# An expert's second product in two accumulations side by side, and the result stored in three pieces

## The chip, the cores and the metric
One core of a Trainium2 chip runs the kernel. The metric is the device time of one execution in microseconds. Three executions of the kernel before took 155.20, 155.12 and 154.73 us, a median of 155.12.

## The reference
Two mixture-of-experts layers over 1024 rows of 128 numbers (8 batches of 128). The change lies in the second layer's sparse part. Cut to what matters:

```python
def _L1_ffn_ref(x, Wg, W1, b1, W2, b2):
    xt = x.reshape(n, h)                       # n = 1024 rows of h = 128
    S = sigmoid(xt @ Wg).T                     # 8 experts x 1024 scores
    G, I = top_k(S, k)                         # k = 256 rows for each expert
    ex = xt[I]
    hid = gelu(einsum('ekh,ehf->ekf', ex, W1) + b1[:, None, :], approximate=False)
    out = (einsum('ekf,efh->ekh', hid, W2) + b2[:, None, :]) * G[..., None]
    return zeros_like(xt).at[I].add(out)       # rows of several experts are summed

x = x + _L0_ffn_ref(_L0_cond_ref(x, cond_8, ...), ...)    # first layer
x = x + _L1_ffn_ref(_L1_cond_ref(x, cond_8, ...), ...)    # second layer
```

W1 is 128 x 512 and W2 is 512 x 128 for each expert. All is float32.

## The kernel before
The program is written for each engine by hand, with semaphores between the engines. The first layer and the second layer's conditioning come first; the change touches only what comes after them.

**The second layer's experts.** Each expert takes 256 rows (CAP). Experts 0 to 6 are sparse (SPARSE = 7): their rows are gathered. Expert 7 is dense: it is computed for all 1024 rows in four units of 256 rows (HEAD = 4). `unit` lists these four and then the seven sparse experts, so sparse expert e is unit 4 + e, and the last is unit 10 (UNITS = 11).

For a sparse expert, GpSimd (POOL) gathers the rows into xg in two indirect DMAs (`gather1`, line 448). TensorE turns them (`turn_xg`), ScalarE (ACT) copies them to xgT, and TensorE makes the first product in `up1(n, h)` (line 649): h = 0 gives chunks 0 and 1 of the 512 hidden numbers, h = 1 chunks 2 and 3, each chunk one matmul with 256 columns. ACT applies the gelu to each chunk and writes h1T (line 935), and counts h1T_ready up by one for each chunk. `down_e(n, h)` (line 732) is the second product: for one half h of the 256 rows it waits until h1T_ready says that all four chunks are there, and adds four products, one for each chunk, in one bank. (The profile counts each of these float32 products as two matmuls, so an expert's second product is 16 of them, and an up1 is 4.) The bank comes from `y_bank`, which goes round banks 6, 7 and 1 for the sparse experts. The last matmul of each half counts y1_sent up.

On VectorE (DVE) `score(e, h)` (line 1280) waits for y1_sent, scales a half by its gate and adds the bias, writes y1 and counts y1_kept up. y1_kept tells TensorE that a bank is free and POOL that the half can be stored.

**Where the halves go.** The sparse experts have 14 halves. The first ten (SCATTERS = 10, experts 0 to 4) are written by indirect DMAs from POOL into zeroed planes in DRAM (`add`, line 455), one plane for each expert, and SP loads each plane back as soon as both halves are in it (line 407); VectorE adds the five planes to the result x1 (`take_part`, line 1299, five sums over 1024 columns). The last four halves (SPREADS = 4, experts 5 and 6) go by TensorE: VectorE and ACT split y1 in three bfloat16 parts in turns (`thirds_of`, line 1289, and ACT's loop at line 987), and `spread_out` (line 752) multiplies them with one-hot matrices, 24 matmuls for each half, summed in banks 5 (chunks of rows 0 to 3) and 3 (chunks 4 to 7).

**Order on the engines.** TensorE, for n from 5 to 10: turn the rows of expert n - 3, up1(n, 0), then both halves of down_e(n - 1), then up1(n, 1). For n = 10 both up1 come ahead of down_e(9). After the loop come down_e(10) and spread_out. ACT takes xgT and the gelus in the order of the units. VectorE goes through the experts, for each the bias, two scores, and from expert 5 on the thirds; after expert 0 it adds the dense expert, after expert 2 it makes the one-hot matrices, after expert 4 it takes planes 0 and 1, and after expert 6 planes 2, 3 and 4. Then it adds the two banks, one sum over 512 columns for each (line 1341), and each sum counts out_ready up. SP waits for out_ready and stores one half of the result each time (line 410 on; the helper `load` stands at line 357 in the profile), 256 KB in rows of 512 bytes.

Of the kernel before, what the change touches and what calls it, by code (L numbers as in the profile page):

```python
# [24 lines left out]
P = 128  # L25
T, C = 1024, 128
NC = T // P
# [3 lines left out]
NF = F // P  # L31
# [9 lines left out]
NH = CAP // P  # L41
ROW = C + E
SPARSE = 7
# [14 lines left out]
ALU = mybir.AluOpType  # L58
# [55 lines left out]
def adaln_moe(nc, xT, x, first, second, rows, w1, w2, cond_w, gate_w, v1, c1, v2, consts, out):  # L114
    with ExitStack() as ctx:
# [12 lines left out]
        bank = [ctx.enter_context(nc.psum_tensor(f"bank{i}", [P, 512], F32)) for i in range(8)]  # L128
# [19 lines left out]
        v2_sb = sb("v2_sb", [P, E, NF, C])  # L148
# [6 lines left out]
        def const(name):  # L155
# [78 lines left out]
        x1 = c_tok  # L234
# [43 lines left out]
        h1T = sb("h1T", [P, 2, NF, CAP])  # L278
# [47 lines left out]
        xg_turned, xgT_ready, h1_ready, h1T_ready, gb_ready, y1_kept, y1_sent = (sem(n) for n in (  # L326
            "xg_turned", "xgT_ready", "h1_ready", "h1T_ready", "gb_ready", "y1_kept", "y1_sent"))
# [5 lines left out]
        yd_kept = sem("yd_kept")  # L333
# [3 lines left out]
        GATHERS_AHEAD = SPARSE  # L337
        SCATTERS = NH * SPARSE - SPREADS
        SUM_BANKS = (5, 3)

        CHUNKS = T // CAP
        HEAD = DENSE * CHUNKS
# [5 lines left out]
        def y_bank(n, h):  # L348
            return 6 + n % 2 if n < HEAD else (6, 7, 1)[(NH * (n - HEAD) + h) % 3]
# [5 lines left out]
        def _(sp):  # L355
            def load(dst, src, s):
                sp.dma_start(dst, src).then_inc(s, 16)
# [49 lines left out]
            for e in range(PLANES):  # L407
                sp.wait_ge(added[e], 16 * min(NH, SCATTERS - NH * e))
                load(part[e], plane[e].rearrange("(p c) d -> p (c d)", p=P), part_in[e])
            for g in range(2):  # L410
                sp.wait_ge(out_ready, g + 1)
                load(out.rearrange("(c p) d -> p c d", p=P)[:, 4 * g:4 * g + 4], x1[:, 4 * g:4 * g + 4], out_done)
            sp.wait_ge(out_done, 32)


        @block.gpsimd
# [59 lines left out]
        def _(pe):  # L476
# [255 lines left out]
            def down_e(n, h):  # L732
                dense, e, q = unit[n]
                pe.wait_ge(h1T_ready, 4 * (n + 1))
                if n == 0:
                    pe.wait_ge(row_ready, NC)
                if n == 1:
                    pe.wait_ge(sc_ready, 2)
                if 2 <= n < HEAD:
                    pe.wait_ge(yd_kept, n - 1)  # L740
                if n == HEAD:
                    pe.wait_ge(yd_kept, HEAD)
                if n == HEAD + 1 and h == 0:
                    pe.wait_ge(idx1_ready, SPARSE)
                if NH * (n - HEAD) + h >= 3:
                    pe.wait_ge(y1_kept, NH * (n - HEAD) + h - 2)
                for f in range(NF):
                    mm = pe.matmul(bank[y_bank(n, h)][:, C * h:C * h + C], h1T[:, n % 2, f, P * h:P * h + P],  # L748
                                   v2_sb[:, e, f], start=(f == 0), stop=(f == NF - 1))
                mm.then_inc(y1_sent, 1)  # L750

            def spread_out():
                for n in range(SPREADS):
                    pe.wait_ge(spread_ready, n + 1)
                    pe.wait_ge(last_third, n + 1)
                    for c in range(NC):
                        for k in range(3):
                            mm = pe.matmul(bank[SUM_BANKS[c // 4]][:, P * (c % 4):P * (c % 4) + P],
                                           spread1h[n][:, P * c:P * c + P], thirds[:, n, k],
                                           start=(n == 0 and c % 4 == 0 and k == 0),  # L760
                                           stop=(n == SPREADS - 1 and c % 4 == 3 and k == 2))
                        if n == SPREADS - 1 and c % 4 == 3:
                            mm.then_inc(summed, 1)
# [39 lines left out]
            for n in range(HEAD + 1, UNITS):  # L803
                e = n - HEAD
                if e + 1 < SPARSE:
                    turn_xg(e + 1)
                up1(n, 0)
                if n == HEAD + 1:
                    find_slots(SPARSE - 1)
                if n == UNITS - 1:  # L810
                    up1(n, 1)
                for h in range(NH):
                    down_e(n - 1, h)
                if n < UNITS - 1:
                    up1(n, 1)
            for h in range(NH):
# [4 lines left out]
        def _(act):  # L821
# [161 lines left out]
            def y1_of(n):  # L983
                e, h = (SCATTERS + n) // NH, (SCATTERS + n) % NH
                return y1[:, e % Y1_RING, h]

            for n in range(0, SPREADS, NH):
                for m in range(n, n + NH):
                    act.wait_ge(y1_kept, SCATTERS + m + 1)
                    act.activation(thirds[:, m, 0], y1_of(m), ACT.Copy).then_inc(first_third, 1)  # L990
                for m in range(n, n + NH):
                    act.wait_ge(first_left, m + 1)
                    act.activation(thirds[:, m, 1], left[:, m], ACT.Copy).then_inc(second_third, 1)


        @block.vector
        def _(v):
# [338 lines left out]
                    take_part(1)  # L1336
            for e in range(2, PLANES):
                take_part(e)
            for g in range(2):
                v.wait_ge(summed, g + 1)  # L1340
                v.tensor_tensor(acc[:, 512 * g:512 * g + 512], acc[:, 512 * g:512 * g + 512], bank[SUM_BANKS[g]][:],
                                ALU.add).then_inc(out_ready, 1)

# [46 lines left out]
```

## Time and profile before

| | us |
|---|---|
| median of the runs (154.73 to 155.20) | 155.12 |
| profiled execution, its own time | 154.64 |
| its span, first to last instruction | 152.8 |
| TensorE matmul busy | 139.7 (91%) |
| TensorE weight load busy | 121.2 (79%) |
| VectorE busy | 93.4 (61%) |
| ScalarE busy | 84.2 (55%) |
| GpSimd busy | 57.7 (38%) |

The table is one profiled execution. Matmuls are pipelined, so TensorE's busy share isn't its share of the peak. A busy share is an average over stages with different limits; which engine leads in a stage is read from the chain of waits, in which each piece of work is followed back to what released it.

### The profile page before, as it was taken

To read this page: it belongs to the slowest core of one execution; us is meant where nothing else is said; L and a number is where in the kernel's file an instruction comes from. 1 tells how busy PE (TensorE), PEld (TensorE's weight loads), DVE (VectorE), ACT (ScalarE), POOL (GpSimd) and SP (SyncE) were. 2 spreads that over 40 slices of the span, in tenths; PEclk is the share of its full clock that TensorE was granted. 3 is DMA by queue.
4 is the path that set the end of the run, shared out by engine and by line. 5 is a ranking of instruction groups with operands and counts; after the bars stand their busy time and mean duration, and the time that the engine had idled before them with its cause. 6 is when DMAs were issued, how large, how long until landed. Compare 5 with 4: busy or idle time off the path is not lost.

```text
span 152.8 us, 3654 instructions
## 1 busy us (share of the span) xinstructions
PE 139.7 (91%) x1132; PEld 121.2 (79%) x1132; DVE 93.4 (61%) x314; ACT 84.2 (55%) x255; POOL 57.7 (38%) x62
## 2 busy tenths in 40 slices
PE   7999698899999999999799997979997999999980
PEld 3848688799999999964589975748975988889970
DVE  0278947756655555450599777765541694737891
ACT  0497708667777765620367869985226244457500
POOL 0000277344477555561500000002587787773000
PEclk9999999999999999999999999999999999999999
DMA  5995417999999992112702950030022221567604
GB/s 149 328 408 202 129 44 230 381 353 361 397 398 321 266 317 68 34 56 71 223 0 92 401 200 0 0 150 2 18 55 55 59 57 53 189 191 222 225 8 137
DMA packets 13877, 26.16 MB, mean 171 GB/s; under 512 B 1970, under 2 KB 7474, under 8 KB 13474
## 3 DMA queue, kind: packets, MB, share of 16 engines
q1 hardware_dynamic: 11010, 21.73, 41.0%
q0 software_dynamic: 1760, 3.67, 7.8%
q10 hardware_dynamic: 1088, 0.52, 1.2%
q8 instruction: 10, 0.16, 0.4%
q14 instruction: 9, 0.07, 0.2%
HBM read 19.98 MB, written 5.93 MB: 170 GB/s over the span
## 4 chain that ended last, share of the span: by engine, by line
PE 62%; DVE 18%; issue 5%; DMA 5%; POOL 4%; ACT 2%; DVEq 2%; POOLq 0%
PE bank L580 12%; PE bank L590 12%; PE bank L748 10%; PE bank L659 10%; POOL xg L452 3%; PE bank L626 3%; PE bank L482 3%; DVE c_tok L1301 2%; PE bank L635 2%; DMA xg<-rows,idx 2%; DVE y L1071 2%; DMA picked<-y,sidx 1%; DMA got<-picked 1%; DVE hid L1166 1%; PE bank L505 1%
## 5 line engine op out<-in xcount | busy, mean ns | idle before, releaser
L858 ACT ACTIVATE hT<-bank,w_now 128x128 f32<-128x128 f32 x92 | 26.3, 369 | 12.9 <-PE bank L580 12.9
L580 PE MATMUL bank<-xg,w_now 128*128 (+1 forms) x184 | 24.7, 277 | 1.3 <-ACT xg L851 0.7
L430 POOL DMA_INDIRECT xs<-rows,gidx x15 | 14.8, 987 | 28.0 <-DVE gidx L1078 17.7
L935 ACT ACTIVATE h1T<-bank,c_sb 128x256 f32<-128x256 f32 x44 | 18.2, 472 | 12.5 <-PE bank L659 12.4
L590 PE MATMUL bank<-w_sb,hT 128*128 (+1 forms) x184 | 24.4, 276 | 0.3 <-ACT hT L858 0.3
L580 PEld LDWEIGHTS bank<-xg,w_now 128*128 128x128 f32 x184 | 22.4, 192 | 2.4 <-issue 1.8
L590 PEld LDWEIGHTS bank<-w_sb,hT 128*128 128x128 f32 x184 | 22.4, 192 | 0.5 <-ACT hT L858 0.5
L748 PE MATMUL bank<-v_sb,h1T 128*128 128x128 f32 x176 | 22.7, 280 | 0.0
L748 PEld LDWEIGHTS bank<-v_sb,h1T 128*128 128x128 f32 x176 | 20.9, 192 | 1.4 <-ACT h1T L935 1.2
L435 POOL DMA_INDIRECT picked<-y,sidx x16 | 15.8, 986 | 10.2 <-DVE y L1127 9.3
L452 POOL DMA_INDIRECT xg<-rows,idx x14 | 14.2, 1016 | 5.7 <-issue 3.7
L659 PE MATMUL bank<-xgT,v_sb 128*128 128x256 f32 x56 | 14.2, 381 | 0.0
L1121 DVE TENSOR_TENSOR yt<-bank,b_sb 128x128 f32<-128x128 f32 x23 | 6.7, 292 | 12.1 <-PE bank L590 9.7
L482 PE MATMUL bank<-ones 128*128 128x512 bf16 x44 | 12.1, 418 | 1.1 <-DVE ones L1014 1.1
L463 POOL TENSOR_TENSOR hlfv<-hlf1h,cst 128x128 bf16<-128x128 bf16 x1 | 0.8, 778 | 30.7 <-DVE hlf1h L1252 30.7
L1095 DVE COPY w_now<-w_sb 128x516 f32 (+1 forms) x23 | 11.1, 483 | 1.5 <-DVE exi L1082 1.0
L1127 DVE SCALAR_TENSOR_TENSOR y<-yt,pairm,y 128x128 f32 (+1 forms) x23 | 8.1, 351 | 5.4 <-DVE yt L1121 5.3
L459 POOL DMA_INDIRECT plane<-x_sb,idx x10 | 9.9, 994 | 3.1 <-issue 3.1
L659 PEld LDWEIGHTS bank<-xgT,v_sb 128*128 128x128 f32 x56 | 9.7, 191 | 0.8
L482 PEld LDWEIGHTS bank<-ones 128*128 128x128 bf16 x44 | 4.8, 112 | 5.4 <-issue 1.1
L1285 DVE SCALAR_TENSOR_TENSOR x_sb<-bank,xg,gb 128x128 f32<-128x128 f32 x14 | 4.7, 349 | 7.0 <-PE bank L748 7.0
L659 PE MATMUL bank<-w_eff,v_sb 128*128 128x256 f32 x32 | 8.9, 390 | 0.0
(202 smaller groups left out, 229.6 us busy)
## 6 DMA issues: line engine op xcount, KB each, us to landing
v_sb<-in_v SPq DMA_DIRECT2D x16, 256.0 KB
cw_sb<-in_cond_w SPq DMA_DIRECT2D x8, 386.5 KB, 5.2
plane<-y SPq DMA_DIRECT2D x5, 512.0 KB, 5.0
w_sb<-plane SPq DMA_DIRECT2D x5, 512.0 KB, 3.8
w_sb<-in_w SPq DMA_DIRECT2D x2, 1024.0 KB, 8.6
w_sb<-in_w SPq DMA_DIRECT2D x1, 1290.0 KB, 7.7
w_sb<-in_w SPq DMA_DIRECT2D x1, 774.0 KB, 4.5
rows<-row SPq DMA_DIRECT2D x1, 544.0 KB, 2.9
```

The source lines that it names most:

```text
L430: pool.indirect_dma_start(out=xs[:, b % RING], out_offset=None, in_=rows0, in_offset=rows_at(gidx, b)).then_inc(gathered[b % RING], 16)
L435: pool.indirect_dma_start(out=picked, out_offset=rows_at(sidx, b), in_=y0[:, b], in_offset=None).then_inc(scattered, 16)
L452: pool.indirect_dma_start(out=xg[:, i], out_offset=None, in_=rows1, in_offset=rows_at(idx1, i)).then_inc(gathered1[e], 16)
L459: pool.indirect_dma_start(out=plane[e], out_offset=rows_at(idx1, i), in_=y1[:, e % Y1_RING, h], in_offset=None).then_inc(added[e], 16)
L482: pe.matmul(out_bank[:], ones[:], ones[:].unsqueeze(1).to_broadcast([P, 4, P]), start=True, stop=True)
L580: mm = pe.matmul(bank[2 + j % 2][:, P * f:P * f + P], w1_now[:, j % WB_RING, P * f:P * f + P], xsT[:, bass.ds((j - e) * P, P)], start=True ...
L590: mm = pe.matmul(bank[6 + j % 2][:, 0:C], hT[:, j % 2, P * f:P * f + P], w2_sb[:, bass.ds(e * (NF * C) + f * C, C)], start=(f == 0), stop= ...
L659: mm = pe.matmul(bank[UP_BANKS[u % 4]][:, CAP * f:CAP * f + CAP], v1_sb[:, e, P * fc:P * fc + P], rows_in, start=True, stop=True)
L748: mm = pe.matmul(bank[y_bank(n, h)][:, C * h:C * h + C], h1T[:, n % 2, f, P * h:P * h + P], v2_sb[:, e, f], start=(f == 0), stop=(f == NF ...
L858: ins = act.activation(hT[:, j % 2, P * f:P * f + P], bank[2 + j % 2][:, P * f:P * f + P], ACT.Relu, bias=w1_now[:, j % WB_RING, F + f:F + ...
L935: act.activation(h1T[:, n % 2, fc], bank[UP_BANKS[(2 * n + h) % 4]][:, CAP * f:CAP * f + CAP], ACT.Gelu, bias=c1_sb[:, e * NF + fc:e * NF ...
L1095: v.tensor_copy(w1_now[:, j % WB_RING], w1_sb[:, bass.ds(e * FW, FW)]).then_inc(w1_now_ready, 1)
```

## The change
In the loop over the sparse experts the two calls of down_e(n - 1) are replaced by one call of a new function `down_both(n - 1)`, for units 4 to 9 (experts 0 to 5). It waits for the first two chunks of h1T, multiplies chunks 0 and 1 for row half 0 and then for row half 1, each in its own bank, then waits for the other two chunks, and multiplies chunks 2 and 3 for both halves in the same two banks. Both banks are awaited ahead of their first matmul. The last unit keeps down_e.

The result is stored in three pieces, chunks 0 to 3 (256 KB), 4 and 5 (128 KB), 6 and 7 (128 KB). VectorE's second sum is cut in two of 256 columns accordingly. SP stores the first and the last piece, ACT the middle one.

```diff
--- before.py
+++ after.py
@@ -337,6 +337,7 @@
         GATHERS_AHEAD = SPARSE
         SCATTERS = NH * SPARSE - SPREADS
         SUM_BANKS = (5, 3)
+        OUT_PIECES = [(0, 4), (4, 6), (6, NC)]
 
         CHUNKS = T // CAP
         HEAD = DENSE * CHUNKS
@@ -407,10 +408,11 @@
             for e in range(PLANES):
                 sp.wait_ge(added[e], 16 * min(NH, SCATTERS - NH * e))
                 load(part[e], plane[e].rearrange("(p c) d -> p (c d)", p=P), part_in[e])
-            for g in range(2):
-                sp.wait_ge(out_ready, g + 1)
-                load(out.rearrange("(c p) d -> p c d", p=P)[:, 4 * g:4 * g + 4], x1[:, 4 * g:4 * g + 4], out_done)
-            sp.wait_ge(out_done, 32)
+            for g, (c0, c1_) in enumerate(OUT_PIECES):
+                if g != 1:
+                    sp.wait_ge(out_ready, g + 1)
+                    load(out.rearrange("(c p) d -> p c d", p=P)[:, c0:c1_], x1[:, c0:c1_], out_done)
+            sp.wait_ge(out_done, 16 * len(OUT_PIECES))
 
 
         @block.gpsimd
@@ -748,6 +750,25 @@
                     mm = pe.matmul(bank[y_bank(n, h)][:, C * h:C * h + C], h1T[:, n % 2, f, P * h:P * h + P],
                                    v2_sb[:, e, f], start=(f == 0), stop=(f == NF - 1))
                 mm.then_inc(y1_sent, 1)
+
+            def down_both(n):
+                e = unit[n][1]
+                pe.wait_ge(h1T_ready, 4 * n + 2)
+                if n == HEAD:
+                    pe.wait_ge(yd_kept, HEAD)
+                if n == HEAD + 1:
+                    pe.wait_ge(idx1_ready, SPARSE)
+                for g in range(2):
+                    if g == 1:
+                        pe.wait_ge(h1T_ready, 4 * n + 4)
+                    for h in range(NH):
+                        if g == 0 and NH * (n - HEAD) + h >= 3:
+                            pe.wait_ge(y1_kept, NH * (n - HEAD) + h - 2)
+                        for f in (2 * g, 2 * g + 1):
+                            mm = pe.matmul(bank[y_bank(n, h)][:, C * h:C * h + C], h1T[:, n % 2, f, P * h:P * h + P],
+                                           v2_sb[:, e, f], start=(f == 0), stop=(f == NF - 1))
+                        if g == 1:
+                            mm.then_inc(y1_sent, 1)
 
             def spread_out():
                 for n in range(SPREADS):
@@ -809,8 +830,7 @@
                     find_slots(SPARSE - 1)
                 if n == UNITS - 1:
                     up1(n, 1)
-                for h in range(NH):
-                    down_e(n - 1, h)
+                down_both(n - 1)
                 if n < UNITS - 1:
                     up1(n, 1)
             for h in range(NH):
@@ -984,6 +1004,11 @@
                 e, h = (SCATTERS + n) // NH, (SCATTERS + n) % NH
                 return y1[:, e % Y1_RING, h]
 
+            def store(g):
+                c0, c1_ = OUT_PIECES[g]
+                act.wait_ge(out_ready, g + 1)
+                act.dma_start(out.rearrange("(c p) d -> p c d", p=P)[:, c0:c1_], x1[:, c0:c1_]).then_inc(out_done, 16)
+
             for n in range(0, SPREADS, NH):
                 for m in range(n, n + NH):
                     act.wait_ge(y1_kept, SCATTERS + m + 1)
@@ -991,6 +1016,7 @@
                 for m in range(n, n + NH):
                     act.wait_ge(first_left, m + 1)
                     act.activation(thirds[:, m, 1], left[:, m], ACT.Copy).then_inc(second_third, 1)
+            store(1)
 
 
         @block.vector
@@ -1336,10 +1362,11 @@
                     take_part(1)
             for e in range(2, PLANES):
                 take_part(e)
-            for g in range(2):
-                v.wait_ge(summed, g + 1)
-                v.tensor_tensor(acc[:, 512 * g:512 * g + 512], acc[:, 512 * g:512 * g + 512], bank[SUM_BANKS[g]][:],
-                                ALU.add).then_inc(out_ready, 1)
+            for g, (c0, c1_) in enumerate(OUT_PIECES):
+                v.wait_ge(summed, c0 // 4 + 1)
+                o = C * (c0 % 4)
+                v.tensor_tensor(acc[:, C * c0:C * c1_], acc[:, C * c0:C * c1_],
+                                bank[SUM_BANKS[c0 // 4]][:, o:o + C * (c1_ - c0)], ALU.add).then_inc(out_ready, 1)
 
 def kernel(x, cond_8, L0_cond_W_base, L0_cond_b_base, L0_cond_As, L0_cond_Bs, L0_ffn_router_w, L0_ffn_w1,
            L0_ffn_b1, L0_ffn_w2, L0_ffn_b2, L1_cond_W_up, L1_cond_b_up, L1_cond_W_gate, L1_cond_b_gate,
```

## Rows read from the trace of the kernel before

**Rows 1.** Page: span, and granted TensorE clock in tenths over 40 slices.
```profile
span 152.8 us, 3654 instructions
PEclk9999999999999999999999999999999999999999
```

**Rows 2.** Chain of waits from 110 us (start, us, what): second products.
```profile
119.14 1.89 PE bank L748 x16
...
122.98 1.96 PE bank L748 x16
...
134.70 1.96 PE bank L748 x16
136.66 2.59 PE bank L659 x12
139.25 1.80 PE bank L748 x16
```

**Rows 3.** Waits, 112 to 153 us: total us, times, longest.
```profile
PEld bank L748 <- ACT h1T L935: 1.2, 4, 0.3
```

**Rows 4.** Timeline, 121.5 to 125.6: start, us, [idle before <- releaser].
```profile
121.99 0.84 ACT L935 ACTIVATE h1T<-bank,c_sb 128x256 f32<-128x256 f32 x2 [2.35 <-PE bank L659]
...
122.88 1.86 PEld L748 LDWEIGHTS bank<-v_sb,h1T 128*128 128x128 f32 x16 [0.31 <-ACT h1T L935]
```

**Rows 5.** Chain of waits from 110 us: VectorE at the end.
```profile
141.17 0.36 DVE x_sb L1285
...
144.62 1.23 DVE c_tok L1301
...
148.40 0.69 DVE c_tok L1341
```

**Rows 6.** Timeline, 139 to 143 us, VectorE: score (5,0), remainder, last third.
```profile
140.27 0.35 DVE L1285 SCALAR_TENSOR_TENSOR x_sb<-bank,xg,gb 128x128 f32<-128x128 f32 x1 [0.22 <-PE bank L748]
...
141.44 0.28 DVE L1292 TENSOR_TENSOR w_sb<-x_sb,w_sb 128x128 f32<-128x128 f32 x1
...
142.10 0.28 DVE L1295 TENSOR_TENSOR w_sb<-w_sb 128x128 bf16<-128x128 f32 x1
```

**Rows 7.** Timeline of TensorE, 112 to 153 us: the spreading product.
```profile
142.66 2.84 PE L758 MATMUL bank<-w_sb,y 128*128 128x128 bf16 x48
145.34 2.84 PE L758 MATMUL bank<-w_sb,hT 128*128 128x128 bf16 x48
```

**Rows 8.** Timeline, 133 to 139 us: plane load, score, last indirect store.
```profile
133.72 0.32 SPq L357 DMA_DIRECT2D w_sb<-plane  x1
...
136.79 0.35 DVE L1285 SCALAR_TENSOR_TENSOR x_sb<-bank,xg,gb 128x128 f32<-128x128 f32 x1 [0.54 <-PE bank L748]
...
138.22 0.97 POOL L459 DMA_INDIRECT plane<-x_sb,idx  x1 [0.30 <-issue]
```

**Rows 9.** Line 357, 125 to 153 us: issue ns, starts, landing of all.
```profile
L357 SPq DMA_DIRECT2D w_sb<-plane x5: 319/320/320, 130.1 to 141.6; - x5
...
DMA to landing us min/median/max: 2.4/3.4/4.3
```

**Rows 10.** Tile out_x: its stores, issue ns, first and last start, landing.
```profile
L357 SPq DMA_DIRECT2D out_x<-c_tok x2: 389/389/389, 149.1 to 149.7; - x2
...
DMA to landing us min/median/max: 2.4/2.5/2.6
```

**Rows 11.** Stretches of the store: five engines' busy, clock, DMA share, GB/s.
```profile
150.50:151.00 0.50, 0.00 (x0) 0.00 (x0) 0.00 (x0) 0.00 (x0) 0.00 (x0) 1.00 1.03 297
...
151.50:152.00 0.50, 0.00 (x0) 0.00 (x0) 0.00 (x0) 0.00 (x0) 0.00 (x0) 1.00 0.76 220
```

**Rows 12.** A stretch of the loads of got, same columns.
```profile
74.00:74.50 0.50, 0.50 (x4) 0.14 (x2) 0.35 (x1) 0.28 (x1) 0.50 (x1) 1.00 1.05 316
```

**Rows 13.** DMA issues, 70 to 76 us: KB each, us to landing.
```profile
got<-picked SPq DMA_DIRECT2D x1, 128.0 KB, 2.8
got<-picked ACTq DMA_DIRECT2D x1, 128.0 KB, 3.1
```

## The prediction, made before the change was run

> **What bounds the kernel now.** I read the page first, then the chain of waits from 110 us on, then the timeline of the stretch in which the sparse experts run, then the store. The span is 152.8 us and TensorE runs at its higher level, 2.4 GHz, throughout [rows 1], so no clock change has to be priced. From 117.4 to about 142.7 us TensorE leads: the chain alternates between the first product (up1, line 659) and the second (down_e, line 748) of one sparse expert after another. In [rows 2] the reader should compare the second products with each other. Sixteen matmuls take 1.80 us when nothing holds them (expert 5 at 139.25), and 1.96 us for experts 1 to 4; the first and the last of these four stand there. The view of waits gives the reason [rows 3]: four times the weight load of line 748 stood idle, 0.3 us each, until ACT had written h1T. [rows 4] is one such place: the gelu pair for chunks 2 and 3 starts at 121.99, lasts 0.84, ends at 122.83, and the weight load starts at 122.88. down_e waits for all four chunks before its first matmul, though it begins with chunk 0. Expert 5's product has both up products of expert 6 ahead of it (12 matmuls at 136.66), and there the gelu is done in time.
>
> From 141 us on the lead passes to VectorE [rows 5]: the score of row half (5,1) at 141.17, the splitting into thirds, the scores and thirds of expert 6, three sums of the planes from 144.62, then the two sums with the banks from 148.40, and the store. TensorE ends its spreading product (line 758) at 148.18 [rows 7]. The first bank is complete half of the last row half's 24 matmuls earlier, near 147.5, and VectorE asks for it at 148.40. So TensorE has about 0.8 us to spare at the end, and VectorE has none.
>
> **Part 1, down_both for experts 0 to 5.** It has the same 16 matmuls and 16 weight loads per expert, and the same number of waits on TensorE's queue (two for h1T, two for a free bank), in another order: chunks 0 and 1 for both row halves, then a wait for the gelu's second pair, then chunks 2 and 3 for both. Expert 6 keeps down_e.
> - Removed: the 0.16 us (1.96 less 1.80) in each of four experts, 0.64 us in all [rows 2]. In the chain the whole loss is inside these rows.
> - Does the wait come back at the middle? The first eight matmuls take half of 1.80, 0.90 us. They would start at about 122.7 and end at 123.6; chunks 2 and 3 are written at 122.83 [rows 4]. The second wait has nearly 0.8 us of cover, and costs nothing. The other three experts are alike. Queued behind that wait are the remaining eight matmuls and then up1 of the next expert; nothing else would be held.
> - Two accumulations open in two banks at once: the trace of before has none. Its nearest rows bound a change of bank. The last two experts' products follow each other through three such changes and end where 1.80 us each has them: nothing. Expert 0's product, which follows matmuls of another kind, takes 1.89 [rows 2]: 0.09 us at most for one change. Below nothing I exclude, since the matmuls already run at an even 0.11 us. There are two changes more for each of six experts, 12 in all: 0 to 1.08 us. I take 0, from the row with the same instruction and the same banks, and keep the other end for the range.
> - The first row half is complete four matmuls (0.45 us) before the second, where it was eight (0.90). Who waits for it? VectorE's score, and behind that the indirect stores on POOL. Those run back to back: the last is issued at 138.22, though its score began at 136.79 and took 0.35 [rows 8]. So POOL has about 1.1 us to spare there, keeps its times, and sets when the planes can be loaded.
> - At the last changed expert (5) the thirds hang on this. Before: score (5,0) at 140.27, (5,1) at 141.17, and the first remainder at 141.44 right behind it [rows 5, 6]. The remainder also needs ACT's copy of (5,0), 0.32 us. With the half 0.45 later relative to TensorE's end, that score would run from 140.72 to 141.07 on the old clock and the copy to 141.43, just in time for 141.44. The second half's chain doesn't change, and with it the first last third at 142.10 [rows 6], ahead of the spreading product at 142.66 [rows 7]. I charge nothing. If the cover were gone, the price is what the copy is late, up to 0.1 us, and TensorE's own end has 0.8 to spare.
> - What is late next? The plane loads keep their times, since POOL does. Plane 1's is issued at 133.72 [rows 8]; with the longest landing of 4.3 us [rows 9] it is in by 138.0. The second of two sums of 1.23 behind score (4,1) takes it, near 138.4 now (136.79 + 0.35 + 1.23) and 137.8 then. A wait of 0.2 us there falls into VectorE's idle time before score (5,0). Plane 4 is issued at 141.6 and in by 145.9 [rows 9]; its sum starts at 147.1 now (two sums of 1.23 behind 144.62 [rows 5]) and would at 146.5. There is 0.6 us of room left, so the gain isn't cut, but a gain above 1.2 us would be.
> Part 1 gives 0.64 us.
>
> **Part 2, the store in three pieces.** Now two stores of 256 KB go out from SP at 149.1 and 149.7 and land 2.4 to 2.6 us later [rows 10]. While they run, the DMA engines are busy all the time, 1.03 at 297 GB/s, and the last data pass near 151.9 [rows 11]. 512 KB (524 thousand bytes) at about 290 GB/s are 1.8 us, so the data began to flow near 150.1, 0.9 us after the first issue, and never paused. The end of the store is set by the start of the first piece and by the rate, not by the last piece. The first piece, four chunks, is unchanged: same sum (0.69 us [rows 5]), same issue. The second sum is cut in two of 256 columns. One of 512 takes 0.69 and one of 128 takes 0.28 [rows 6], so one of 256 takes about 0.42 (estimate from the two), and the second of them ends about 1.34 us after the first sum starts instead of 1.29. SP issues the last piece 0.05 later. Its data could flow 0.9 later again, 0.7 after the first data; by then some 200 of the 384 KB ahead of it have passed, and the rest is its cover. Piece 1 goes out from ACT, whose last work are the copies for the thirds; nothing is queued behind it there. Cost of the cut: 0, and 0.05 if that cover were gone.
> What two queues do to the rate is not shown for stores. The nearest rows are the loads of got on SP and ACT together, also of 512-byte rows: 316 GB/s at a share of 1.05 [rows 12]. By that row 512 KB would take 0.15 us less. Against it, the ACT queue's 128 KB landed after 3.1 us where SP's took 2.8 [rows 13], which bounds the loss at 0.3. I take 0, because one queue already keeps the engines at a share of 1.03, and keep both ends for the range.
> The Trainium skill speaks to this: its page "DMA: Bandwidth & Descriptors", section "Rules for kernel authors", says that spreading DMAs over the issuing engines doesn't raise bandwidth, as all of them run on the same 16 DMA engines, and saves issue time only. By that rule Part 2 gives 0; by the row it would give 0.15. The trace agrees as far as it goes, with its full share on one queue; no row shows stores on two.
>
> **The sum.** Span 152.8 less 0.64 is 152.16. The profiled execution took 154.64 us, 1.84 more than its span, so it would take 154.00. It lay 0.48 below the median of the runs (155.12), and at the median the same step gives **154.5 us**.
>
> **The rivals.**
> - Two queues move the store faster: 0.15 more, 154.33. For it, 316 against 297 GB/s; against it, the full share on one queue, and that those were loads.
> - The time doesn't move, 155.1. The gap ahead of the second product would have to be something else than the gelu, or VectorE would have to wait for its own chain. Against it: in [rows 4] the gelu's end and the load's start are 0.05 apart, and the one product with a longer lead has no gap. For it: VectorE, ACT and TensorE hand over some ten times in the last 12 us, and any 0.1 us in each of those uses up the gain.
> - Slower: changing the bank between open accumulations costs TensorE time in every expert. Its price is 12 changes at up to 0.09, 1.08 us, which less the 0.64 gives 155.55. It cancels the gain at 0.05 for a change, and makes the kernel slower by 0.3% from 0.09 ((0.64 + 0.47) / 12). For it only expert 0's 1.89; against it the evenly paced last 32 matmuls.
>
> **How the numbers follow.** A measurement of this kernel tells about 0.3%, 0.47 us, from no change; the bound lies at 154.65, close to the forecast. The forecast has a chance of 0.60, and as 0.64 is only 0.17 above the bound, 0.45 of that counts as faster and 0.15 as the same. The faster store has 0.17 (0.16 faster, 0.01 same), no movement 0.15 (all the same), and the costly bank change 0.08 (0.06 slower, 0.02 same). That makes faster 0.61, same 0.33, slower 0.06. The range takes in the faster store with the spread of the runs (0.4 below the median) at 153.9, and no movement at 155.15; it leaves out most of the bank case and a little below.
>
> **What the profile after would show.** Right: the waits of line 748's weight load for ACT's h1T are gone, each second product takes 1.80 in the chain, the spreading starts near 142.0, the plane sums start near 144.0, and the data of the store flow for 1.8 us. The plane loads keep their times. Wrong in part 1: second products of more than 1.85 us with nothing waited for (bank changes), or the same gap now at chunk 2. Wrong at the end: plane sums that begin with a wait for a plane, or a TensorE that finishes after 148. Wrong in part 2: over 300 GB/s in the store (faster), or a last piece that lands later than 3.2 us after the first issue (slower).

## The result and the profile after

The changed kernel took 154.83 us in the median of 20 runs, the kernel before 155.10 in 20 runs of its own. The ratio is 0.9959, 95% interval 0.9939 to 0.9978, so 0.41% or 0.64 us less (0.34 to 0.95). A few executions of most kernels are some 2 us or more longer than the fastest of the same kernel; they are left out of every ratio here and below, and with them the traces of three kernels whose profiled execution was one of these. The profiled execution of the changed kernel took 154.17 us, its span 152.4.

The two spans, 152.8 and 152.4, can't be set against each other as they stand. Part of their difference arises ahead of everything that was changed. A mark that both kernels pass in the same state is the turning of expert 2's rows, the last place where TensorE waits for a gather. TensorE's timeline, first before and then after (start us, us, engine, line, operation, [idle before <- what ended it]):

```profile
117.40 0.44 PE L729 MATMUL bank<-cst,xg 128*128 128x128 f32 x2 [1.10 <-DMA xg<-rows,idx]
```
```profile
117.06 0.44 PE L731 MATMUL bank<-cst,xg 128*128 128x128 f32 x2 [0.88 <-DMA xg<-rows,idx]
...
141.63 2.84 PE L779 MATMUL bank<-w_sb,y 128*128 128x128 bf16 x48
144.31 2.84 PE L779 MATMUL bank<-w_sb,hT 128*128 128x128 bf16 x48
```

So 0.34 us of the 0.4 were there at the mark. Counted from it, the spreading product starts after 24.57 us where it started after 25.26 (142.66 in [rows 7]): 0.69 less. But the end of the span comes after 35.34 us where it came after 35.40. In this execution TensorE's gain is all there, and the kernel as a whole got 0.06 us of it. The chain of waits of the changed kernel shows where it stayed (start us, us, what):

```profile
span 152.4 us, 3650 instructions
```
```profile
118.80 1.89 PE bank L768 x16
...
122.64 1.78 PE bank L768 x16
...
126.38 1.80 PE bank L768 x16
...
138.40 4.62 DMA plane<-x_sb,idx
143.02 0.02 issue
143.04 3.62 DMA w_sb<-plane
...
146.75 1.24 DVE c_tok L1327
147.99 0.02 issue
148.01 0.69 DVE c_tok L1368
```

The second products are line 768 now. The ones that took 1.96 us in [rows 2] take 1.78 to 1.80, and the view of waits has no row for a weight load on h1T, which answers [rows 3]. The end, though, is led by another chain than in [rows 5]: the last indirect store, the load of plane 4, and then the sum that takes it, at 146.75. VectorE stood idle ahead of that sum. The waits of the same stretch, 112 to 153 us (total us, times, longest):

```profile
DVE c_tok L1327 <- DMA w_sb<-plane: 1.1, 2, 0.7
```

Before, no sum of a plane waited. The timeline of POOL and VectorE shows the other new thing (before first, as a continuation of [rows 8], then after):

```profile
136.95 0.97 POOL L459 DMA_INDIRECT plane<-x_sb,idx  x1 [0.31 <-issue]
137.06 2.48 DVE L1301 TENSOR_TENSOR c_tok<-c_tok,w_sb 128x1024 f32<-128x1024 f32 x2
```
```profile
136.04 1.22 DVE L1327 TENSOR_TENSOR c_tok<-c_tok,w_sb 128x1024 f32<-128x1024 f32 x1
136.64 1.45 POOL L461 DMA_INDIRECT plane<-x_sb,idx  x1 [0.30 <-issue]
137.70 1.23 DVE L1327 TENSOR_TENSOR c_tok<-c_tok,w_sb 128x1024 f32<-128x1024 f32 x1 [0.44 <-DMA w_sb<-plane]
138.40 1.36 POOL L461 DMA_INDIRECT plane<-x_sb,idx  x1 [0.30 <-issue]
```

The last two indirect stores take 1.45 and 1.36 us, where they took 0.97. Before, each was issued about 0.1 us ahead of a plane sum (the first in the lines shown; the last at 138.22 in [rows 8], with the second of the two sums at 138.3); after, each starts in the middle of one.

The store (stretches; five engines' busy time, clock, DMA share, GB/s) is as full as in [rows 11] and no faster, with two queues on it:

```profile
150.00:150.50 0.50, 0.00 (x0) 0.00 (x0) 0.00 (x0) 0.00 (x0) 0.00 (x0) 1.00 1.00 284
150.50:151.00 0.50, 0.00 (x0) 0.00 (x0) 0.00 (x0) 0.00 (x0) 0.00 (x0) 1.00 1.02 293
```

### The profile page after: what moved, and what is told of

Same layout as the page of the kernel before. It is cut to its first block, busy times and chain, and to the rows that moved or that the text cites. A ratio compares the mean times of both kernels' runs of the same rounds, so it can differ in the third digit from the quotient of the medians.

```text
span 152.4 us, 3650 instructions
## 1 busy us (share of the span) xinstructions
PE 138.9 (91%) x1132; PEld 121.5 (80%) x1132; DVE 93.5 (61%) x315; ACT 84.3 (55%) x255; POOL 58.5 (38%) x62
## 3 DMA queue, kind: packets, MB, share of 16 engines
q0 software_dynamic: 1760, 3.67, 8.0%
## 4 chain that ended last, share of the span: by engine, by line
PE 54%; DVE 16%; DMA 10%; POOL 8%; issue 6%; DVEq 2%; POOLq 1%; ACT 1%
PE bank L582 12%; PE bank L592 12%; PE bank L661 6%; POOL plane L461 4%; PE bank L768 4%; POOL xg L454 3%; DMA plane<-x_sb,idx 3%; PE bank L628 3%; PE bank L484 3%; PE bank L750 3%; DMA w_sb<-plane 2%; PE bank L637 2%; DMA xg<-rows,idx 2%; DVE y L1097 2%; DMA picked<-y,sidx 1%
## 5 line engine op out<-in xcount | busy, mean ns | idle before, releaser
L461 POOL DMA_INDIRECT plane<-x_sb,idx x10 | 10.8, 1085 | 3.0 <-issue 2.7
```

The source lines that it names most:

```text
L461: pool.indirect_dma_start(out=plane[e], out_offset=rows_at(idx1, i), in_=y1[:, e % Y1_RING, h], in_offset=None).then_inc(added[e], 16)
```

## The experiments

Each kernel was timed beside the kernel before on the same chip; ratios are to that kernel, with 95% intervals, and 0.1% is 0.155 us. The intervals are 0.2 to 0.4% to either side, because the executions of any of these kernels spread over more than 1 us. A good part of that arises ahead of the changed code: the mark above is passed between 117.06 and 118.66 us in the traces. So the traces, counted from the mark, tell apart what the times can't. Each is a single execution, though, and shows what happened in it, not how often that happens.

### Which part of the change brings the gain

Only down_both:

```diff
-        OUT_PIECES = [(0, 4), (4, 6), (6, NC)]
...
-            store(1)
...
-            for g, (c0, c1_) in enumerate(OUT_PIECES):
+            for g in range(2):
```

> down_both for experts 0 to 5, the store left as before (two pieces from SP). Theory A (the gelu waits are the gain, the store adds nothing): 0.4 to 0.65 us below before, like the whole change. Theory B (the store in pieces brings a good part): 0.3 us or less below before. In the trace both expect second products of 1.80 us without a wait for h1T.

Measured: 0.9946 (0.9906 to 0.9985).

Only the store in pieces:

```diff
-                down_both(n - 1)
+                for h in range(NH):
+                    down_e(n - 1, h)
```

> down_e as before, the store in three pieces over two queues. Theory A: within 0.1 us of before, data of the store flowing 1.8 us as before. Theory B: 0.15 to 0.4 us below before.

Measured: 0.9982 (0.9953 to 1.0011). down_both alone reaches the whole gain or more: 0.84 us less (0.23 to 1.46), where theory B allowed 0.3. The store alone isn't told from nothing: 0.28 us less, but the interval goes from 0.17 us more to 0.73 less. That point lies in theory B's range and not in A's, so this run by itself doesn't decide. The trace of the changed kernel speaks for A: its rate is 284 to 293 GB/s at a share of 1.00 to 1.02, and from the issue of the first store to the end of the span it took 3.67 us (148.73 to 152.4) where it was 3.69 before (149.11 to 152.8).

### Does plane 4 keep back part of the gain?

```diff
+            sp.wait_ge(part_in[PLANES - 1], 16)
             sp.wait_ge(out_done, 16 * len(OUT_PIECES))
...
-            for e in range(2, PLANES):
+            for e in (2, 3, 3):
                 take_part(e)
```

SP's wait at its end keeps the load of plane 4 inside the execution; VectorE has none for it.

In the changed kernel:

> The changed kernel, but VectorE adds plane 3 a second time in place of plane 4, so its last plane sum waits for no load; POOL, SP and all transfers are as before, and the sum takes the same time. Theory P (in the changed kernel the indirect stores on POOL and the load of plane 4 now end last and keep back part of the gain): 1.0 to 1.3 us below before, 0.5 to 0.7 below the changed kernel. Theory Q (the 0.68 us wait in the one trace of the changed kernel is an exception): as the changed kernel, 0.4 to 0.65 below before.

and in the kernel before:

> The kernel before with the same edit: plane 3 added twice, no wait for plane 4. Its trace shows no wait for plane 4. Theory P and the forecast's 0.6 us of room: 0 to 0.15 us below before. If before loses as much to the plane as the changed kernel does: 0.4 us or more below before.

Measured: 0.9935 (0.9902 to 0.9968) and 0.9982 (0.9954 to 1.0009). Without the wait the changed kernel is 1.0 us below before (0.5 to 1.5), which is theory P's lower bound; the interval takes in theory Q too. The kernel before is 0.28 us lower without the wait (0.14 higher to 0.71 lower), between its two forecasts, 0 to 0.15 and 0.4 or more. It didn't wait for plane 4 in its trace to begin with, and the traces end 35.45 us after the mark with the edit and 35.40 without.

The trace of the edited changed kernel ends 34.70 us after the mark, but this isn't the work of the edit. In this execution the load of plane 4 was issued at 142.0 and landed 3.3 us later, at 145.3, and VectorE began its last plane sum at 146.2. The unedited kernel wouldn't have waited there either. So the trace shows what an execution with plane 4 in time looks like, and the claim that the wait costs the changed kernel something on average rests on the times. Their intervals overlap with the changed kernel's own 0.9959, which is from another set of runs.

The changed kernel again:

> The changed kernel itself, on the chip of the three others. All theories: 0.3 to 0.8 us below before. Theory L: the last two indirect stores take 1.3 us or more again; theory V: they may be back at 0.97.

Measured: 0.9995 (0.9969 to 1.0021). That is 0.08 us less, where all theories had 0.3 to 0.8, though the interval reaches 0.48. In these 12 runs no gain is to be seen, and together with the 20 runs before, the gain of the changed kernel is somewhere between nothing and 0.9 us. Its trace had the stalled stores again, and yet no wait for plane 4:

```profile
137.63 1.22 DVE L1327 TENSOR_TENSOR c_tok<-c_tok,w_sb 128x1024 f32<-128x1024 f32 x1
138.24 1.45 POOL L461 DMA_INDIRECT plane<-x_sb,idx  x1 [0.30 <-issue]
139.41 1.23 DVE L1327 TENSOR_TENSOR c_tok<-c_tok,w_sb 128x1024 f32<-128x1024 f32 x1 [0.56 <-DMA w_sb<-plane]
139.99 1.48 POOL L461 DMA_INDIRECT plane<-x_sb,idx  x1 [0.30 <-issue]
```

It passed the mark at 118.66 and ended at 153.3, 34.64 us later: 0.76 less than before from the mark on, though its span is longer. So the stall recurs, the gain behind the mark is there when plane 4 is in time, and whether it is in time changes from one execution to the next. (In this one it landed at 147.4, 0.3 us before VectorE asked for it.)

### What holds up POOL's stores

The sums of planes 0 and 1 in four pieces each:

```diff
+                if e < 2:
+                    for o in range(0, T, 256):
+                        ins = v.tensor_tensor(acc[:, o:o + 256], acc[:, o:o + 256], part[e][:, o:o + 256], ALU.add)
+                    link(ins)
+                else:
                     link(v.tensor_tensor(acc, acc, part[e], ALU.add))
```

> The changed kernel with the sums of planes 0 and 1 cut in four sums of 256 columns each. Theory L (a plane sum, with both inputs in SBUF, holds up an indirect store that POOL starts while it runs; the two last stores took 1.45 and 1.36 us instead of 0.97 since down_both moved the sums): the last two indirect stores take at most 1.2 us, plane 4 lands 0.5 us or more earlier than in the changed kernel, time 0.2 to 0.5 us below it. Theory V (their length varies by itself or through the DMA rings): still 1.3 us or more, time as the changed kernel or up to 0.2 above it for VectorE's added work.

A maximum in place of each of the two sums, with one input from SBUF:

```diff
+                if e < 2:
+                    link(v.tensor_reduce(lg2[:, :, 0], part[e].rearrange("p (c d) -> p c d", c=NC), AX.X, ALU.max))
```

> The changed kernel with the sums of planes 0 and 1 replaced by a maximum over the same plane (one input from SBUF, nearly the same length), so two planes are missing in the result. Theory L: the last two indirect stores are back at 0.97 us, though VectorE is as busy beside them. Theory V: still 1.3 us or more in one or both.

And the kernel before, with its sums moved so that they meet a store:

```diff
                 if e == 4:
+                    v.wait_ge(part_in[0], 16)
+                    link(v.tensor_reduce(lg2[:, :, 0], part[0][:, 0:256].rearrange("p (c d) -> p c d", c=NC), AX.X, ALU.max))
                     take_part(0)
```

> The kernel before, with a maximum over 256 columns of plane 0 (about 0.4 us, one input from SBUF) ahead of the sums of planes 0 and 1, so that these start 0.4 us later and the last indirect store begins inside one. Theory L: the last indirect store takes 1.2 to 1.5 us where it took 0.97. Theory V: 0.97, as in all traces with down_e so far.

Measured in the traces, timelines of the three kernels in this order:

```profile
137.53 1.42 DVE L1329 TENSOR_TENSOR c_tok<-c_tok,w_sb 128x256 f32<-128x256 f32 x4
138.15 0.97 POOL L461 DMA_INDIRECT plane<-x_sb,idx  x1 [0.30 <-issue]
139.41 1.48 DVE L1329 TENSOR_TENSOR c_tok<-c_tok,w_sb 128x256 f32<-128x256 f32 x4 [0.46 <-DMA w_sb<-plane]
139.43 0.97 POOL L461 DMA_INDIRECT plane<-x_sb,idx  x1 [0.30 <-issue]
```
```profile
136.87 1.21 DVE L1328 TENSOR_REDUCE lg<-w_sb 128x8 f32<-128x1024 f32 x1
137.49 0.97 POOL L461 DMA_INDIRECT plane<-x_sb,idx  x1 [0.30 <-issue]
138.48 1.22 DVE L1328 TENSOR_REDUCE lg<-w_sb 128x8 f32<-128x1024 f32 x1 [0.40 <-DMA w_sb<-plane]
138.76 0.96 POOL L461 DMA_INDIRECT plane<-x_sb,idx  x1 [0.30 <-issue]
```
```profile
137.28 0.97 POOL L459 DMA_INDIRECT plane<-x_sb,idx  x1 [0.31 <-issue]
...
137.84 2.49 DVE L1301 TENSOR_TENSOR c_tok<-c_tok,w_sb 128x1024 f32<-128x1024 f32 x2
138.56 1.34 POOL L459 DMA_INDIRECT plane<-x_sb,idx  x1 [0.32 <-issue]
```

All three came out as theory L says for the length of the stores. With one input the instruction is just as long and begins just as far ahead of the store (0.62 us; in the changed kernel 0.60), and the store takes 0.97. In the kernel before, the store that is issued ahead of the sums keeps its 0.97 and the one that starts inside the first takes 1.34. The stall can be reckoned from what was left of the sum: 137.26 less 136.64 is 0.62 in the changed kernel and the store is 0.48 longer; 0.53 and 0.39 for its second; 0.50 and 0.37 in the shifted kernel before. Each time it is the rest of the sum less about 0.14 us. The same holds for all eleven stores that start inside a 1024-column sum in the six traces of the table below that have them: the difference is 0.12 to 0.14 us, with the store between 1.34 and 1.69.

The maximum differs from the sum in two things, though: it reads one input, and it writes 8 numbers for each row where the sum writes 1024. And one input isn't always harmless. An earlier store of the changed kernel starts while VectorE makes two one-hot matrices, each from one 1024-column input:

```profile
129.53 0.88 DVE L1295 TENSOR_SCALAR hT<-y,idx1f 128x1024 bf16<-128x1024 int16 x2
130.04 1.21 POOL L461 DMA_INDIRECT plane<-x_sb,idx  x1 [0.30 <-issue]
```

It takes 1.21 us, and 1.15 to 1.21 in the same place in every trace. So the kind of instruction counts, and these runs don't show which of its properties.

The Trainium skill gives a reason for the sum: by its page "SBUF — State Buffer", section "Who interferes with whom", a VectorE instruction with two SBUF inputs takes its second one through the read interface that it shares with GpSimd, so that a GpSimd instruction that reads SBUF has to wait, and the order of issue decides who waits. These traces agree with it where the sum is first. Where the store is first, by 0.1 us, no wait shows on either side: the store keeps its 0.97 us, and the two sums behind it take 2.48 together, 1.24 each.

The times are less clear. The small sums took 0.9979 (0.9947 to 1.0011), the maximum 0.9937 (0.9911 to 0.9963), the shifted kernel before 0.9976 (0.9943 to 1.0009). The small sums are 0.16% below the changed kernel on the same chip, inside the intervals, though their trace ended 34.64 us after the mark. That is 0.25 us, as theory L forecast, but no more than these times scatter by. In the trace plane 4 was in 28.5 us after the mark, against 29.6 and 28.7 in the two traces of the changed kernel. The shifted kernel does more work than before and had no reason to be faster; with the store alone and the kernel before without the plane wait it is the third that lies 0.2% low. A difference of 0.2% in these times says nothing.

The maximum shows another thing. Its stores weren't held up, and still plane 4 came 29.6 us after the mark and VectorE waited 0.66 us for it, as in the first trace of the changed kernel. So the wait comes without the stall too.

### Why the store's data take so long

```diff
             for e in range(PLANES):
                 sp.wait_ge(added[e], 16 * min(NH, SCATTERS - NH * e))
+                if e not in (2, 3):
                     load(part[e], plane[e].rearrange("(p c) d -> p (c d)", p=P), part_in[e])
...
-            for e in range(2, PLANES):
-                take_part(e)
+            for e in (0, 1, 4):
+                take_part_again(e)
```

> The changed kernel without the loads of planes 2 and 3; VectorE adds planes 0 and 1 once more in their place, so two planes are missing in the result. From its issue on POOL to the issue of plane 4's load on SP the last indirect store has taken 2.8 to 5.2 us in the traces so far, in both kernels. Theory C (the 512 KB loads of planes 2 and 3 hold up its data on the DMA engines): 2.8 us or less here, plane 4 is in before VectorE asks, and the time is 0.4 us or more below the changed kernel, with fewer long executions. Theory R (it varies by itself): anything from 2.8 to 5.2, and no clear change in time.

Measured: 0.9966 (0.9935 to 0.9996). The last store took 3.0 us to the issue of plane 4's load, of which 1.69 were its own, stalled issue (139.98 to 143.0), and plane 4 was in time. That lies between the theories. Less the stall of 0.72 it is 2.3 us, but the second trace of the changed kernel, with all loads present, has the same: 2.8 less 0.51. Against theory C, the load of plane 1 took 5.1 us with only plane 0's load and scattered rows beside it, longer than any in [rows 9]. And in the kernel with the maximum, all loads present, it had been 5.2 us from store to load with an unstalled issue. The scatter between 2.8 and 5.2 us stays open.

### A version meant to beat both

The sums with the banks ahead of plane 4's, and that one in pieces (cut to the lines that are new; the loop over the planes ends at plane 3, and `last` is plane 4 in SBUF):

```diff
+            for g in range(2):
+                v.wait_ge(summed, g + 1)
+                link(v.tensor_tensor(acc[:, 512 * g:512 * g + 512], acc[:, 512 * g:512 * g + 512], bank[SUM_BANKS[g]][:], ALU.add))
+                if g == 0:
+                    v.wait_ge(part_in[PLANES - 1], 16)
+                for c0, c1_ in OUT_PIECES:
+                    if c0 // 4 == g:
+                        v.tensor_tensor(acc[:, C * c0:C * c1_], acc[:, C * c0:C * c1_],
+                                        last[:, C * c0:C * c1_], ALU.add).then_inc(out_ready, 1)
```

> The changed kernel with another order at VectorE's end: the sums with the two banks come before the sum of plane 4, which is cut like the result (512, 256, 256 columns), each piece stored at once. If plane 4 ends last, as theory P says, its wait is filled with a bank's sum and the first store leaves 0.7 us earlier or more: 0.8 to 1.2 us below the changed kernel. If VectorE's own chain ended last: 0.4 to 0.7 us below, through the earlier first store alone.

and with the small sums as well:

> Both edits together, the small sums of planes 0 and 1 and the late sum of plane 4 in pieces. Theory L with P: 0.2 us or more below the late sum alone. Theory V: the same as the late sum alone.

Measured: 0.9981 (0.9960 to 1.0002) and 0.9989 (0.9958 to 1.0020). The first is 0.14% or 0.2 us below the changed kernel on the same chip, where 0.4 or more was expected by either theory, so it missed. The second is no faster than the first, as theory V has it, but 0.2 us couldn't have been seen here. The trace of the first shows part of the reason:

```profile
146.94 0.69 DVE L1368 TENSOR_TENSOR c_tok<-c_tok,bank 128x512 f32<-128x512 f32 x1 [0.51 <-PE bank L779]
147.66 0.69 DVE L1373 TENSOR_TENSOR c_tok<-c_tok,w_sb 128x512 f32<-128x512 f32 x1
```

A bank's sum in front of plane 4's waits for TensorE's spreading product instead, 0.51 us. One late neighbour was exchanged for the other, and the span ended 34.80 us after the mark. In this execution the exchange paid: plane 4's load was issued at 143.4 and took 4.2 us, so it was in at 147.6, and in the changed kernel's order VectorE would have asked for it near 146.4 and waited 1.2 us (an estimate from these two). Where the plane is in time, the same order costs the 0.51 and brings nothing back.

Plane 4 first, in halves, each followed by its bank's sums and their stores, together with the small sums of planes 0 and 1 (cut in the same way):

```diff
+            v.wait_ge(part_in[PLANES - 1], 16)
+            for g in range(2):
+                cols = slice(512 * g, 512 * g + 512)
+                link(v.tensor_tensor(acc[:, cols], acc[:, cols], last[:, cols], ALU.add))
+                v.wait_ge(summed, g + 1)
+                for c0, c1_ in OUT_PIECES:
+                    if c0 // 4 == g:
+                        o = C * (c0 % 4)
+                        v.tensor_tensor(acc[:, C * c0:C * c1_], acc[:, C * c0:C * c1_],
+                                        bank[SUM_BANKS[g]][:, o:o + C * (c1_ - c0)], ALU.add).then_inc(out_ready, 1)
```

> A version meant to be faster than both: the changed kernel with the small sums of planes 0 and 1, and at the end the sum of plane 4 in two halves, each followed at once by the sums with its bank and their stores. The first 256 KB go out 0.65 us earlier in VectorE's chain, the last piece at the same time as in the changed kernel. If the rate of the store sets the end, as in the forecast: 0.4 to 0.6 us less than with small sums alone, about 0.9 to 1.2 below before. If the last piece's own latency sets it: no more than 0.1 us less than with small sums alone.

Measured: 0.9941 (0.9907 to 0.9976), 0.9 us below before, a median of 153.99 us. Its trace passed the mark at 118.20 and ended 34.3 us later, 0.34 less than with small sums alone (just under what was expected if the rate sets the end) and 1.1 less than before. It is faster than the kernel before. That it is faster than the changed kernel isn't shown by the times: the intervals of 0.9941 and 0.9959 overlap. The traces say so, 34.3 us against 34.64 and 35.34, which is one execution against two. In its timeline neither TensorE nor plane 4 is waited for:

```profile
147.25 0.69 DVE L1374 TENSOR_TENSOR c_tok<-c_tok,w_sb 128x512 f32<-128x512 f32 x1
147.98 0.69 DVE L1379 TENSOR_TENSOR c_tok<-c_tok,bank 128x512 f32<-128x512 f32 x1
148.58 0.68 DVE L1374 TENSOR_TENSOR c_tok<-c_tok,w_sb 128x512 f32<-128x512 f32 x1
...
149.30 0.75 DVE L1379 TENSOR_TENSOR c_tok<-c_tok,bank 128x256 f32<-128x256 f32 x2
```

The first store leaves at 148.69, 30.49 us after the mark, where it was 31.03 with the small sums alone. Of the kernels that compute the whole result it has the lowest ratio, not told apart from down_both alone (0.9946). 256 KB flow while the second half is still being summed, so that the DMA engines have a gap before the other pieces instead of a queue. Whether cutting the second half in two has any part in this wasn't tested.

```profile
150.00:150.50 0.50, 0.00 (x0) 0.00 (x0) 0.05 (x1) 0.00 (x0) 0.00 (x0) 1.00 0.99 287
150.50:151.00 0.50, 0.00 (x0) 0.00 (x0) 0.00 (x0) 0.00 (x0) 0.00 (x0) 1.00 0.66 178
```

The traces together. "Stores" are the lengths of the last two indirect stores on POOL; "plane 4 in" is when its load has landed and "end" the end of the span, both counted from the mark:

| kernel | mark, us | stores, us | plane 4 in, us | wait for plane 4, us | end, us |
|---|---|---|---|---|---|
| before | 117.40 | 0.97, 0.97 | 28.5 | none | 35.40 |
| before, plane 3 twice | 118.35 | 0.97, 0.97 | 29.4 | none | 35.45 |
| before, sums shifted | 117.73 | 0.97, 1.34 | 28.9 | none | 35.37 |
| changed | 117.06 | 1.45, 1.36 | 29.6 | 0.68 | 35.34 |
| changed, again | 118.66 | 1.45, 1.48 | 28.7 | none | 34.64 |
| changed, plane 3 twice | 117.20 | 1.44, 1.58 | 28.1 | none | 34.70 |
| small sums | 118.56 | 0.97, 0.97 | 28.5 | none | 34.64 |
| maximum for sums | 117.89 | 0.97, 0.96 | 29.6 | 0.66 | 35.31 |
| banks ahead of plane 4 | 117.40 | 1.45, 1.43 | 30.2 | none, 0.51 for TensorE | 34.80 |
| two loads less | 118.65 | 1.45, 1.69 | 27.6 | none | 34.65 |
| plane 4 in halves | 118.20 | 1.19, 1.16 | 28.6 | none | 34.30 |

VectorE asks for plane 4 after 29.7 us with down_e and after 29.0 with down_both. With VectorE's order at the end unchanged, the kernels with down_both end after 34.64 to 34.70 us where the plane is in by then, and after 35.31 and 35.34 where it comes 0.6 us later. The gain of 0.7 us is there or not there as the plane is in time or late, with stalled stores and without.

## Why the prediction was right, and where it wasn't

The forecast was 154.5 us from 155.12, 0.62 less; the ratio gives 0.64 less in the first comparison. The size fits, but the steps under it that gave plane 4 its room failed, and that the first 20 runs came within 0.02 us of the forecast is partly luck: 12 further runs gave 0.08 us less (0.48 less to 0.33 more).

- **The gain on TensorE, 0.64 us: right.** The four second products went from 1.96 to 1.78 or 1.80, and the spreading product starts 0.69 earlier from the mark. Expert 0's keeps its 1.89, so that this isn't a wait for h1T.
- **Changes of bank at 0: right.** A product with three changes of bank (1.78 to 1.80) runs at the pace of one with a single change (1.80). The slower rival is gone: two changes more at its 0.09 each would have made 1.98 of the 1.80.
- **The second wait, the scores and the thirds at 0: right.** The first plane sum behind the thirds starts at 143.60, 26.54 us after the mark, where it was 27.22 (144.62 in [rows 5]): all of the 0.68 has arrived on VectorE by then.
- **POOL keeps its times: wrong.** The step asked whether POOL would wait for a score, and that costs it nothing: once a score is what released a store (128.75), with the same 0.30 us between stores as ever. It didn't ask what the moved sums do to POOL beside them. From the mark, the last store is issued after 21.34 us instead of 20.82 (138.22 in [rows 8]), 0.52 later, 0.48 of it by the stall of the store ahead of it, and is then itself 0.39 longer.
- **0.6 us of room for plane 4: wrong in size.** Before, it was in 28.5 us after the mark (145.9) and asked for after 29.7. In the changed kernel's trace it was in after 29.6 (143.04 + 3.62) and asked for after 29.0. It came 1.1 later: 0.5 through the later issue, 1.2 (0.39 of it stall) because the store took 4.6 us where it had taken 3.4, less 0.7 for a faster load. The 3.4 was one value of a spread; the traces had 2.8 to 5.2. I had taken the longest landing for the load, and for the store ahead of it the one that this trace happened to show. The 0.6 us was one value too: with plane 3 added twice in the kernel before, plane 4 was in after 29.4 us, which would have been late for a VectorE that asks after 29.0, with no stalled store at all. The sign for this was on record, "plane sums that begin with a wait for a plane", and it came, with 0.68 us.
- **The store at 0: right**, against the row of [rows 12]. Two queues gave 284 to 293 GB/s, and from the first issue to the end it was 3.67 us against 3.69. The share of 1.03 on one queue was the row to go by. The Trainium skill's rule (page "DMA: Bandwidth & Descriptors", section "Rules for kernel authors"), that spreading DMAs over issuing engines doesn't raise bandwidth, is borne out here for stores too. A small slip: by its own figures the data began 1.0 us after the first issue (149.1 to 150.1), not 0.9; no term hangs on it.

Of the rivals, "the time doesn't move" was given a chance of 0.15 through a hand-over chain of VectorE, ACT and TensorE. It takes place, in some executions, through a chain that I had reckoned with and given room: 35.34 against 35.40 us from the mark. That the first 20 runs nevertheless show the forecast gain, and the next 12 none, could come from a gain of 0.7 us that is kept in some executions and lost in others, on top of more than 1 us of spread from elsewhere. This isn't shown: the set with the gain gave the trace without it, and the set without gave the trace with it. How often it is lost isn't known, as each kernel has one trace or two.

## What to carry to other kernels

Before an engine is made to finish earlier, list what its instructions will now run beside. An instruction that was harmless because it began 0.1 us after its neighbour can cost that neighbour 0.4 us when it begins 0.6 us before it. And the room ahead of a transfer is only as good as the longest landing that it can have, over the whole chain from store to load: one trace shows one value. Where the spread of the times is larger than the gain, count from a mark that both kernels pass in the same state.

## What was unexpected of the hardware

- An indirect store on POOL takes 0.97 us beside a VectorE maximum over 1024 columns, and 1.34 to 1.69 when it starts inside a sum of two SBUF operands of that length: longer by the rest of the sum less 0.12 to 0.14 us. Issued 0.1 us ahead of the sum it takes 0.97. In pieces of 256 columns the sum cost it 0 to 0.22 us. Beside the instruction that makes a one-hot matrix, with one 1024-column input, it took 1.15 to 1.21.
- The time from an indirect store's issue to its landing went from 2.8 to 5.2 us for the same store at the same place, with 3.0 in the one trace without two of the loads beside it. Without the stalls it is 2.3 to 5.2. What decides it is open.
